# Two-layer convolution and feed-forward kernel: when the four quarters of the gated z are scaled and split

## What is computed

```python
# L1_ffn, on y (64*64 tokens by 1024), the channel mix of x by agg_w
H = jnp.einsum('btd,od->bto', y, W) + b              # 1024 x 1024
z = jnp.einsum('btd,dr->btr', y, A)                  # rank 32
# anchors: every second token; logits from H[:, anchors, :8] and z @ LiMEs.T, each over its global maximum
weights = probs * sigmoid((probs - second_largest) / 0.5); weights /= weights.sum()
p_mix = weights_full @ LiMEs                         # per token, rank 32
delta = (z * p_mix) @ Bmat * scaling                 # rank 32 to 1024
x = x + H + delta
```

## Time and profile before

| | us |
|---|---|
| median of 3 runs (lowest, highest) | 661.28 (660.92, 662.16) |
| profiled execution, its own time | 660.13 |
| its span, first to last instruction | 658.3 |
| TensorE busy | 634.5 (96%) |
| DVE, ACT, POOL busy | 434.0, 337.4, 334.9 |
| mean granted TensorE clock | 0.99 |

### The profile page before, as it was taken

How to read it: one execution, slowest core, us unless ns; L and a number is a source line. 1 busy time by engine, 2 the same in 40 slices (tenths; PEclk the granted TensorE clock), 3 DMA queues, 4 the chain that set the end, 5 groups by cost and what they waited for, 6 DMA issues and landing times.

```text
span 658.3 us, 15000 instructions
## 1 busy us (share of the span) xinstructions
PE 634.5 (96%) x5853; PEld 342.0 (52%) x5886; DVE 434.0 (66%) x922; ACT 337.4 (51%) x574; POOL 334.9 (51%) x222
## 2 busy tenths in 40 slices
PE   7989999999999999999999997999999999999997
PEld 5565555566666666566554443444444444444443
DVE  5766887888888888888637789644444334444434
ACT  2667988666778777766662336433333233333100
POOL 3001222225888622226484677976666787666500
PEclk9799999999999999999999998999999999999999
DMA  8868878568879898754529011565454433546103
GB/s 300 304 136 309 311 279 307 207 244 292 302 284 344 300 349 313 253 211 156 206 83 351 34 36 65 200 247 192 192 191 145 155 133 144 191 192 241 73 7 128
DMA packets 46628, 138.39 MB, mean 210 GB/s; under 512 B 13156, under 2 KB 13444, under 8 KB 46377
## 3 DMA queue, kind: packets, MB, share of 16 engines
q1 hardware_dynamic: 41806, 120.65, 51.9%
q10 hardware_dynamic: 4752, 16.78, 6.3%
HBM read 89.13 MB, written 48.28 MB: 209 GB/s over the span
## 4 chain that ended last, share of the span: by engine, by line
PE 74%; DVE 3%; issue 1%; ACT 1%; DVEq 0%; ACTq 0%
PE ps L768 36%; PE ps L511 11%; PE ps L452 9%; PE ps L574 7%; PE ps L495 3%; PE ps L750 2%; PE ps L483 2%; PE ps L542 2%; PE ps L545 1%; DVE zT L1531 1%; PE ps L557 1%; ACT wqT L1017 0%; PE ps L522 0%; DVE wqT L1536 0%; PE ps L518 0%
## 5 line engine op out<-in xcount | busy, mean ns | idle before, releaser
L1089 POOL TENSOR_TENSOR x<-x_in,f_both 128x512 f32<-128x512 f32 x64 | 74.0, 1157 | 201.6 <-DVE f_both L1283 201.6
L511 PE MATMUL ps<-wqT,yq_both 128*128 128x512 bf16 x479 | 113.7, 379 | 6.7 <-issue 4.3
L452 PE MATMUL ps<-x_ph,conv_w 64*64 64x256 f32 (+1 forms) x1024 | 97.0, 391 | 0.5 <-DMA conv_w<-in_conv_taps 0.5
L862 ACT ACTIVATE yv<-yb,yinv 128x128 f32<-128x128 f32 x256 | 78.3, 388 | 26.5 <-DVE yinv L1268 26.3
L901 ACT ACTIVATE ring<-ring,ratio 128x2048 f16<-128x2048 f16 x26 | 50.7, 1994 | 60.0 <-DVE x_ph L1546 18.5
L768 PE MATMUL ps<-ffn_wT,ring 128*128 128x512 f16 x312 | 71.6, 379 | 0.0
L511 PEld LDWEIGHTS ps<-wqT,yq_both 128*128 128x128 bf16 x512 | 45.2, 97 | 49.1 <-ACT yq_both L845 1.5
L452 PEld LDWEIGHTS ps<-x_ph,conv_w 64*64 64x64 f32 (+1 forms) x1024 | 51.1, 137 | 35.3 <-issue 14.4
L855 ACT ACTIVATE ring<-ps,t_up 128x512 f16<-128x512 f32 x64 | 40.5, 683 | 47.7 <-issue 39.6
L574 PE MATMUL ps<-ffn_wT,ring 128*128 128x512 f16 x288 | 64.6, 379 | 0.0
L1120 POOL TENSOR_TENSOR bias_b<-ring 128x1024 f32<-128x1024 f16 x13 | 28.6, 2196 | 57.8 <-ACT ring L901 57.7
(11 more groups left out here) (283 smaller groups left out, 1129.7 us busy)
## 6 DMA issues: line engine op xcount, KB each, us to landing
x_ph<-in_x_phases SPq DMA_DIRECT2D x32, 516.0 KB, 6.2
x_in<-in_x SPq DMA_DIRECT2D x32, 512.0 KB, 6.4
x_scratch<-x SPq DMA_DIRECT2D x32, 512.0 KB, 2.8
x_scratch<-ring SPq DMA_DIRECT2D x26, 512.0 KB, 4.1
ring<-x_scratch SPq DMA_DIRECT2D x26, 512.0 KB, 4.3
wst<-in_w_rows SPq DMA_DIRECT2D x12, 512.0 KB, 5.0
x_in<-x_scratch SPq DMA_DIRECT2D x12, 512.0 KB, 6.7
out<-x_in ACTq DMA_DIRECT2D x12, 512.0 KB, 3.5
```

Source lines behind the costliest of these rows:

```text
L452: return mm(ps_conv[o, g * 2 * MB:(g + 1) * 2 * MB], conv_w[k, g, w.start + o.start:w.start + o.stop], xp[k, g, :, view], start=first, sto ...
L511: last = mm(acc_bank(t, h), yqT[:, p, :], wqT[:, p, h * HALF:(h + 1) * HALF], start=p == 0, stop=p == PH - 1)
L862: last = A(yv[:, s, :], yb[:, s, :], ACT.Copy, scale=yinv[:, s:s + 1])
L1089: g.tensor_tensor(x1[:, t % 2, s], x_in[:, t % 3, s], f16[:, s], ALU.add).then_inc(sem("x1_ready"), 1)
```

## The change

On DVE, `fold(4, 0)` goes ahead of the wait for `z_both`. `z_scale(3)` goes ahead of `ends()`. Of the four quarters only the first two are made before the pairs' folds in this order: `z_low(0, 3)`, then `z_scale(0)`; `fold(5, 0)` and `fold(5, 1)` follow at once. `z_low(1, 0)` goes into pair 0 behind `pair_fold(0, 2)`, `z_scale(1)` behind `pair_fold(0, 5)`, `z_scale(2)` and `z_low(2, 1)` to the head of pair 2, `z_low(3, 2)` to the head of pair 3. On ACT, `z_high(1, 0)` goes behind `normalized(8)` and `normalized(9)`, `z_high(2, 1)` behind store 3, `z_high(3, 2)` to the head of j = 2. No instruction is added or removed; TensorE's, POOL's and SP's own programs are the same.

```diff
@@ -1026,11 +1026,9 @@
 
             s_high(0)
             z_high(0, 3)
-            z_high(1, 0)
             normalized(8)
             normalized(9)
-            z_high(2, 1)
-            z_high(3, 2)
+            z_high(1, 0)
             s_high(1)
             store(0)
             store(1)
@@ -1038,10 +1036,13 @@
             normalized(11)
             store(2)
             store(3)
+            z_high(2, 1)
             s_high(2)
             store(4)
             store(5)
             for j in range(1, PAIRS):
+                if j == 2:
+                    z_high(3, 2)
                 store(2 * j + 4)
                 if j + 2 < PAIRS:
                     normalized(2 * j + 10)
@@ -1516,6 +1517,7 @@
             v.tensor_scalar(z_col4[:, 1:2], z_col4[:, 2:3], z_unit[0:NT, 0:1], None, ALU.mult).then_inc(sem("z_top_ready"), 1)
             link(v.tensor_scalar(z_col4[:, 3:4], z_col4[:, 2:3], w_down[0:NT, 0:1], None, ALU.mult))
             fold(3, 1)
+            fold(4, 0)
             dve.wait_ge(sem("z_top_psum"), 2)
             link(v.tensor_scalar(z_both[:, :, :].rearrange("p a t -> p (a t)"), ps_small[:, 128:128 + 2 * NT], 1.0, None, ALU.mult))
 
@@ -1558,18 +1560,12 @@
                 buf = xb(n)[:, h * HALF:(h + 1) * HALF]
                 v.scalar_tensor_tensor(buf, src, unscale[:, t:t + 1], buf, ALU.mult, ALU.add).then_inc(sem("pair_folded"), 1)
 
+            z_scale(3)
             ends()
-            z_scale(3)
+            fold(4, 1)
+            z_low(0, 3)
             z_scale(0)
-            z_low(0, 3)
-            fold(4, 0)
-            z_low(1, 0)
-            fold(4, 1)
-            z_scale(1)
-            z_scale(2)
-            z_low(2, 1)
             fold(5, 0)
-            z_low(3, 2)
             fold(5, 1)
             pair_fold(0, 0)
             add_delta(0, 0)
@@ -1577,14 +1573,21 @@
             pair_fold(0, 1)
             add_delta(2, 0)
             pair_fold(0, 2)
+            z_low(1, 0)
             add_delta(3, 0)
             pair_fold(0, 3, after=3)
             add_delta(4, 0)
             pair_fold(0, 4, after=2)
             add_delta(5, 0)
             pair_fold(0, 5, after=1)
+            z_scale(1)
             pair_fold(0, 6)
             for j in range(1, PAIRS - 1):
+                if j == 2:
+                    z_scale(2)
+                    z_low(2, 1)
+                if j == 3:
+                    z_low(3, 2)
                 pair_fold(j, 0)
                 add_delta(2 * j + 4, 7 * j)
                 pair_fold(j, 1)
```

## The result

The changed kernel takes 654.5 us (median of 4 runs, 654.16 to 655.36), the kernel before beside it 661.1 (4 runs, 660.34 to 662.16): ratio 0.9901, 95% interval 0.9884 to 0.9918, 6.6 us faster. Forecast were 655.3 us and a range of 654.2 to 658.2. A second set of five runs gave 654.2 against 660.41: ratio 0.9895 (0.9877 to 0.9913).

The account below looks back on a forecast made before the run. The prediction took TensorE to bound the kernel, with one stall ahead of product 2 of pair 0. Idle 4.12 plus clock 1.85 gave 5.97 us; 661.28 - 5.97 = 655.3 us, range 654.2 to 658.2.

Parts of the forecast that it names:

- The stall is `fold(5, 0)` late behind the quarters: Pair 0: product 2 waits for fold(5, 0), queued on in-order DVE behind work it doesn't need; removing the stall gains 5.97 us.
- The forecast, 655.3 us: Whole kernel: median of the runs, 661.28 us, less 5.97 us gives 655.3 us; chance 0.78.
- The idle term, 4.12 us: TensorE ahead of product 2 of pair 0: free at 402.49, starts at 406.61, so 4.12 us of waiting is removed.
- the clock term, 1.85 us: Product 2 of pair 0, at lowered clock after the wait: takes 4.44 us instead of 2.59, so 1.85 us is regained.
- The bounds: Gain from the stall: at least 3.95 us if no clock were lost, at most 6.71 with the whole product at half rate.
- Nothing else is late: DVE, POOL, ACT and SP in the new order: every moved or slipped instruction still comes in time for TensorE; cost 0.
- The nearest margin in pair 0 is 2.5 us: DVE in pair 0: add_delta(3) ends at 411.7, TensorE wants it at 414.2; nearest margin claimed as 2.5 us.
- The place in pair 2 has 0.7 us to spare: Head of pair 2 on DVE: pair_fold(2, 0) ends at 444.0, product 3 wants it at 444.8; 0.7 us to spare.
- Nine instructions in front of `fold(5, 0)`: DVE's queue before the change: two row_ends, four z_scale and three z_low stand in front of fold(5, 0), which doesn't need them.
- Stall moved to pair 2: Rival: the tight place ahead of pair_fold(2, 0) fails once by up to 1.9 us, giving 657.2 us; chance 0.13.
- POOL always wins the turn: Rival: DVE is passed over in POOL collisions, TensorE stalls again, 9.1 us in all, giving 664.4 us; chance 0.03.

Follow-up runs that it names:

- experiment 3: The kernel before with fold(5, 0) alone moved up on DVE, ahead of z_scale(1), no quarter moved out: 663.07 us, ratio 1.0046.
- experiment 4: The kernel before with 70 unused small matmuls filling TensorE's wait ahead of product 2 of pair 0: 659.77 us, ratio 0.999.
- experiment 5: The changed kernel with 1, 3 or 5 extra DVE instructions (delays) ahead of pair_fold(2, 0): 654.53, 658.67 and 661.52 us.
- Experiment 8: The changed kernel with z_scale(3) reading its scale from PSUM, not from its copy in SBUF: 655.11 us, one run.

## Why the prediction was right, step by step

- *The stall is `fold(5, 0)` late behind the quarters.* Right as to the instruction that ended the wait; experiment 3 shows that it was one of several late ones. The prediction had followed the whole of DVE's queue, and so held; had it costed only the named wait, it would have called experiment 3 a gain of 6 us where it is a loss of 2.9.
- *The forecast, 655.3 us.* Right, with 654.5. Part of the nearness is luck: the medians gave 6.6 us where 5.97 was forecast, the stretch that the change touches gave 5.80, and the scatter of the part before L737, which the forecast didn't work out, is about 2 us from trace to trace.
- *The idle term, 4.12 us, and the clock term, 1.85 us.* Each can stand, but not both in one sum. 4.12 runs from start to start; in that measure the product took 410.89 - 406.61 = 4.28 us (delta(2) starts at 410.89 in the timeline), and lost 1.69. 4.44 is the chain's figure for a product behind a wait, and goes with the idle 3.96. Either way the sum is 5.81, measured 5.80: 5.97 is 0.16 too much.
- *The bounds.* "3.95 if no clock were lost" was wrong: experiment 4 has no clock loss, and the stretch is 0.09 us shorter only, so without one the change would still have gained 5.7 us. The upper bound, a whole product at half rate (6.71), was nearly reached in one of three traces (6.55).
- *Nothing else is late.* Right in every line but that of pair 0. `fold(4, 0)` used the idle time ahead of `z_both` (1.11 to 0.45 us); `row_ends` end at 392.57, 1.2 us later than before after taking out the 0.45 us by which this trace is behind; `fold(5, 0)` at 397.47 where I had 397.4; `pair_fold(2, 0)` ends at 444.63 where product 3 starts at 445.44.
- *The nearest margin in pair 0 is 2.5 us.* Wrong. By my own times `pair_fold(0, 4)` had less, 417.2 - 415.0 = 2.2. And I let DVE be first and POOL second after `s_low(1)`. In the trace POOL started `x_sums(2)` at 409.34 and DVE came at 409.54, so `z_low(1, 0)` took 3.00 us and `add_delta(3)` ended at 413.99, with delta(5) starting at 414.78: some 0.7 us to spare, as little as in pair 2, though no run tried this place as experiment 5 tried the other. Whoever starts first keeps the other out: 0.2 us decided over 1.8 us (3.00 for 1.22). That this cost nothing was luck.
- *The place in pair 2 has 0.7 us to spare.* Right, by experiment 5 (0.53 us lost of 1.21).
- *Nine instructions in front of `fold(5, 0)`.* They were ten: L1527, 0.34 us, is missing. Nothing hangs on it.
- *The rivals.* "Stall moved to pair 2" didn't come; with 3 and 5 delays it is what would have come. "POOL always wins the turn" is refuted by every collision here in which POOL had more to do: DVE got its turn between two POOL instructions each time (and `z_scale(0)`, which ended at 397.5, before POOL's instruction issued at 396.43 had run).
- The Trainium skill, "SBUF — State Buffer", section "SBUF: two separate sides", puts the collision down to two SBUF inputs of VectorE against a GpSimd instruction. Experiment 8 agrees: 3.04 us with both in SBUF, 1.21 with one in PSUM.

## What to carry to other kernels

When a trace names the instruction that ended a wait on an in-order engine, list what stands behind it too: moving that one ahead only exchanged waits (2.9 us slower here), while moving out the work that isn't due yet gave all of the 5.8 us. Work that is deferred needs a place with room in the loop behind, and the room is the time between the end of the last fold and the matmul that wants the bank: here 0.7 us, past which each microsecond of delay costs one. A cost that shows in a trace, such as a product at half clock, is only worth removing if nothing else would be waited for in the same time.

## What the runs showed of the hardware beyond that

In the chain's figures, where a product behind a wait takes 2.75 us at full clock, the product behind a wait of 4.0 us took 4.44, 5.19 and 4.44 us in three traces of the same kernel. Behind 2.97 us it took 4.14, behind 4.87 us 4.30, and behind 2.62 us 2.75. So a wait of 2.97 us lost the clock, one of 2.62 us in the only trace of it kept it, and a loss cost the product 1.4 to 2.4 us. TensorE kept busy by small matmuls that nothing uses kept its clock both times (70 in 4.07 us and 90 in 5.19).
